# Sums of A quadrants in the output rounds of a fused cross-attention: from GpSimd to VectorE, in the order that the score rounds have

## The reference

```
a = layer_norm(ctx, gamma, beta)
Q, K, V = x @ Wq.T, a @ Wk.T, a @ Wv.T          # split into heads
attn = softmax(mask(Q K^T / sqrt(64)))
out = x + tanh(gate) * ((attn V) @ Wo.T)
```

## Time and profile before

| | |
|---|---|
| median of three executions | 1596.22 us |
| profiled execution, its own time | 1599.35 us |
| its span, first to last instruction | 1597.5 us |
| mean granted TensorE clock | 0.989 |
| TensorE matmuls busy | 1545.4 us (97%) |
| VectorE busy | 1147.4 us (72%), 1298 instructions |
| ScalarE busy | 862.4 us (54%) |
| GpSimd busy | 357.1 us (22%), 254 instructions |
| stretch 890 to 1530 us (640 us) | TensorE 637.35, VectorE 473.20, ScalarE 406.19, GpSimd 241.25 us busy |

### The profile page before, as it was taken

The page is one execution under the profiler, slowest core; times in us unless marked ns, Lnnn a source line. Parts: engine busy times, 40 slices in busy tenths (PEclk is TensorE's granted clock), DMA queues, the critical chain, the costliest instruction groups (busy, mean ns, idle before and its releaser), DMA issues.

```text
span 1597.5 us, 20099 instructions
## 1 busy us (share of the span) xinstructions
PE 1545.4 (97%) x7104; PEld 1254.9 (79%) x7104; DVE 1147.4 (72%) x1298; ACT 862.4 (54%) x1832; POOL 357.1 (22%) x254
## 2 busy tenths in 40 slices
PE   6979999999999999999988999999999999999998
PEld 5756778888888888888766888888888888888887
DVE  8644778686868687878677777777777777777763
ACT  3445444443544354445675666666666666666641
POOL 5323100000000000000132444333344333444321
PEclk9989999999999999999998999999999999999999
DMA  5999864444544453545572444443444534445422
GB/s 212 331 385 387 291 211 157 159 158 158 174 155 173 158 181 135 185 144 172 172 227 87 134 152 152 139 136 115 143 142 150 160 113 129 129 145 158 139 71 87
DMA packets 204578, 271.92 MB, mean 170 GB/s; under 512 B 26688, under 2 KB 92352, under 8 KB 204480
## 3 DMA queue, kind: packets, MB, share of 16 engines
q1 hardware_dynamic: 204480, 270.65, 50.9%
HBM read 161.55 MB, written 105.91 MB: 167 GB/s over the span
## 4 chain that ended last, share of the span: by engine, by line
PE 85%; DVE 8%; DMA 3%; ACT 2%; issue 1%; SPq 1%; POOL 0%; DVEq 0%; ACTq 0%
PE banks L987 27%; PE banks L989 26%; PE banks L988 26%; PE banks L1105 3%; DVE a_ring L847 2%; PE banks L1016 2%; DMA m_scratch<-m_stage 2%; DVE c_out L914 2%; DVE parts L854 1%; DMA xq<-x_t 1%; DVE p_parts L932 1%; ACT probs L683 1%; PE banks L1092 0%; SPq L301 0%; ACT a_ring L638 0%
## 5 line engine op out<-in xcount | busy, mean ns | idle before, releaser
L987 PE MATMUL banks<-parts,a_ring 128*128 128x512 f32 x1792 | 712.4, 398 | 2.9 <-issue 1.8
L989 PE MATMUL banks<-parts,a_ring 128*128 128x512 f32 x1792 | 701.0, 391 | 0.0
L988 PE MATMUL banks<-parts,a_ring 128*128 128x512 f32 x1792 | 700.0, 391 | 0.0
L989 PEld LDWEIGHTS banks<-parts,a_ring 128*128 128x128 f32 x1792 | 337.5, 188 | 72.5
L987 PEld LDWEIGHTS banks<-parts,a_ring 128*128 128x128 f32 x1792 | 338.1, 189 | 70.3 <-issue 2.2
L988 PEld LDWEIGHTS banks<-parts,a_ring 128*128 128x128 f32 x1792 | 338.3, 189 | 67.3
L551 POOL TENSOR_TENSOR probs<-probs,row_rec 128x512 f32<-128x512 f32 x128 | 133.6, 1044 | 1084.4 <-DVE row_rec L928 1084.4
L683 ACT ACTIVATE probs<-probs,neg_max 128x64 f32<-128x64 f32 x1024 | 259.3, 342 | 57.7 <-DVE neg_max L919 57.7
L914 DVE TENSOR_TENSOR c_out<-banks,c_out 128x1024 f32<-128x1024 f32 x160 | 195.5, 1222 | 113.7 <-PE banks L989 109.8
L638 ACT CAST a_ring<-a_sum 128x1024 fp32r<-128x1024 f32 x128 | 134.2, 1048 | 223.2 <-PE banks L989 218.6
L847 DVE TENSOR_TENSOR a_ring<-a_sum,a_ring 128x1024 fp32r<-128x1024 f32 x128 | 185.9, 1452 | 87.5 <-ACT a_ring L638 86.5
(11 more groups left out here) (73 smaller groups left out, 1324.0 us busy)
## 6 DMA issues: line engine op xcount, KB each, us to landing
xq<-x_t SPq DMA_DIRECT2D x32, 1024.0 KB, 5.9
s_scratch<-c_out SPq DMA_DIRECT2D x64, 512.0 KB, 3.1
probs<-s_scratch SPq DMA_DIRECT2D x128, 256.0 KB, 3.1
c_out<-x SPq DMA_DIRECT2D x64, 512.0 KB, 4.6
out<-c_out SPq DMA_DIRECT2D x64, 512.0 KB, 3.1
b_raw<-m_scratch SPq DMA_DIRECT2D x29, 1024.0 KB, 6.6
m_scratch<-m_stage SPq DMA_DIRECT2D x16, 1792.0 KB, 13.1
w_raw<-wk_t SPq DMA_DIRECT2D x16, 256.0 KB, 7.2
```

Source lines behind the costliest of these rows:

```text
L987: pe.matmul(to, wl, mh, start=first, stop=False, skip_group_check=joined)
L988: pe.matmul(to, wh, ml, start=False, stop=False, skip_group_check=joined)
L989: return pe.matmul(to, wh, mh, start=False, stop=last, skip_group_check=joined)
```

## The change

The GpSimd copy of `sum_a` and its four calls go away, and VectorE's calls, which stood under `if n < ROUNDS`, hold for every round. P6, P3 and P7 come right behind `split_a_lo` in the steps of P1, P5 and P6. P5 of an output round comes at the very end of the step of P4, behind the units' work and the `split_b_lo` of that step. `add_out` keeps its place ahead of `split_a_lo` in the output rounds.

```diff
-            def sum_a(n, k):
...
-                nc.gpsimd.tensor_tensor(a_sum[:, A_SUM[k]], *sum_operands(n, k)).then_inc(sum_made, 1)
...
-                if k == P5 and n >= ROUNDS:
-                    sum_a(n, P3)
-                if k == P6 and n >= ROUNDS:
-                    sum_a(n, P7)
...
-                if k == P4 and ROUNDS <= n + 1 < 2 * ROUNDS:
-                    sum_a(n + 1, P5)
-                    sum_a(n + 1, P6)
...
                 if s + 1 < STEPS:
                     split_a_lo(s + 1)
-                if n < ROUNDS:
-                    if k == P1:
-                        sum_a(n, P6)
-                    if k == P5:
-                        sum_a(n, P3)
-                    if k == P6:
-                        sum_a(n, P7)
-                    if k == P4 and n + 1 < ROUNDS:
-                        sum_a(n + 1, P5)
-                    if s > 0:
-                        add_out((s - 1) // 7, (s - 1) % 7)
+                if k == P1:
+                    sum_a(n, P6)
+                if k == P5:
+                    sum_a(n, P3)
+                if k == P6:
+                    sum_a(n, P7)
+                if k == P4 and n + 1 < ROUNDS:
+                    sum_a(n + 1, P5)
+                if s > 0 and n < ROUNDS:
+                    add_out((s - 1) // 7, (s - 1) % 7)
...
                 if s >= 14 * (B - 1) + 6:
                     refill(s)
+                if k == P4 and ROUNDS <= n + 1 < 2 * ROUNDS:
+                    sum_a(n + 1, P5)
```

More of the change, by code:

```diff
@@ L553, in _ @@
             for s in range(14 * (B - 1), STEPS):
-                n, k = s // 7, s % 7
-                if k == P5 and n >= ROUNDS:
-                    sum_a(n, P3)
-                if k == P6 and n >= ROUNDS:
-                    sum_a(n, P7)
                 if s == 103:
```

## The result

The changed kernel is slower by 0.3%, a small difference but clear of the noise in both timings. Timed beside the kernel before, its median was 1602.45 us (6 executions, 1598.98 to 1603.97) against 1597.03 us, the ratio 1.0031 with a 95% interval of 1.0018 to 1.0044. A second timing later gave 1601.94 us against 1597.45, ratio 1.0027 [1.0018, 1.0036], that is +4.3 us (2.9 to 5.7). The forecast had been 1602.1 us, +5.9.

The account below looks back on a forecast made before the run. TensorE was taken as nearly full in the steady rounds, waiting only for VectorE's split L932, with VectorE awaited in the hand-over. Terms 4.5 + 1.4 = +5.9 us on the median 1596.22 gave 1602.1 us, range 1598 to 1607.5.

Parts of the forecast that it names:

- Price of a sum: Each sum moved to VectorE adds 1.14 us to a full queue; 64 sums make 73 us of new VectorE time.
- Term 1, P5 and P6: Steady rounds 17 to 30: P5 fits into waiting for TensorE, P6 replaces L847's wait for GpSimd; cost nothing.
- Term 1, P7: Steady rounds, step of P6: split L932 comes 0.20 us later behind `add_out`, paid in full 14 times, 2.80 us.
- Term 1, P3: Steady rounds, step of P5: next `add_out` 0.08 us late in 11 rounds, more in rounds 18, 20, 25; 1.65 us.
- 4.02, with the sum 5.16: Step of P5: microseconds from L847's start until the next VectorE instruction can start, without and with the sum for P3.
- Term 2: Hand-over from score to output rounds, steps 111 to 114: TensorE's restart in step 114 later by 0.8 to 1.4, taken +1.4 us.
- both stops stay, so I leave it: Hand-over: TensorE's two stops remain, about 4.5 and 4.2 us, so the 5.7 us of low clock was left unchanged.
- VectorE busy: VectorE's busy time was to grow by about 73 us, less some 35 of waits gone.
- win back its waits: Rival, hand-over: VectorE's regained waits count, -1.5 us there, L847 of step 112 before 831 us; 1597.5 us, not slower; 15%.
- The waits did not change sides: Rival: the new queue brings L847 or a sum onto a normalisation, up to 0.5 us in 14 rounds; 1609 us; 5%.
- The low clock did not last longer: Rival, hand-over: first stop grows from 3.25 to 4.5 us, longer low clock costs 3 us more; 1605 us; 8%.
- The rule of the skill: Advice to move work off a saturated VectorE, even to GpSimd; its first half would make the sum larger by 73 us.

Follow-up runs that it names:

- P5 ahead of the pair: Changed kernel with the sum for P5 moved from behind the two Wo splits of the step of P4 to ahead of them: 1598.65 us, ratio 1.0009.

## Why the prediction was right

The direction, the place and the mechanism were right. Two terms were too large, and one of them was argued wrongly. That the time was met within half a microsecond (1602.1 against 1602.45) is partly luck: the sum was 5.9 us, of which the traces show 3.6, and the first timing happened to lie above them.

- *Price of a sum, 1.14 us:* right; L822 starts at 946.46, the sum at 947.59 and L907 at 948.73.
- *Term 1, P5 and P6:* nothing, right; no wait of TensorE appears in their steps.
- *Term 1, P7:* right. The split stands 3.41 us behind `add_out` (forecast 3.42, before 3.22), in each of 14 rounds, so 2.8 us. One sum behind the split takes the whole wait away and one more ahead of it lengthens it by all that the split is later (1.26 us).
- *Term 1, P3:* mis-sized, 1.65 us forecast. All stalls together grew by 3.3 us in the first pair of traces, so P3 is left with some 0.5. The step that was off is "4.02, with the sum 5.16", whose starts came from a queue with gaps. In the full queue of the changed kernel the next instruction can start 5.06 us behind L822 (rounds 22 and 25), and in the other rounds `add_out` stands 5.13 behind it (940.19 to 945.32), 0.63 behind the reduction where 0.57 would do; the 0.06 us fit a wait for TensorE, though the profile lists none. Three rounds were to overrun by more than 0.08; one did, the 25th, whose stall is 1.04 us. The late starts of the `add_out` that opens the step of P5, on which the three rested, are not all the kernel's: in the second profile of the kernel before, its idle time in round 18 is 0.33 us and not 0.98. Only round 25 is late again and again, 1.28, 1.59 and 1.44 us in the three profiles of the changed kernel and 1.25 in the second of the one before. There the 0.7 us of idle time ahead of the next `add_out` takes up most of it; with the sum for P3 in that place it is paid. What `add_out` waits for in that round is open; by the code it can be TensorE or the load of x.
- *Term 2:* its steps were right and its end was not. L822 of step 112 starts 4.61 us behind the pair (forecast 4.6), TensorE's restart in that step comes 1.26 us later (1.26), the pair of step 113 takes 2.85 (2.9), and the restart of step 114 comes 1.32 us later (1.4 taken). The step that did not hold is "both stops stay, so I leave it": the stretch from that restart to the one behind ScalarE's copy took 9.7, 8.2 and 9.8 us in the three traces of the changed kernel, 10.55 and 10.1 in the two of the other, with granted clocks of 0.76 to 1.00. The whole hand-over took 39.8 us in the mean (40.27, 38.77, 40.36) against 39.5 (39.77, 39.27), so nearly all of the 1.32 us was given back. Whether the change shortens this stretch or chance did is open; 1.6 us between executions of one kernel is more than the 0.3 in question.
- *The sum:* 5.9 us forecast. The traces give 3.3 for the rest (737.1 less 733.85, of which the stalls are 3.3) and 0.3 for the hand-over, 3.6 us; the medians gave 5.4 (2.9 to 7.0) and 4.3 (2.9 to 5.7). All agree on 3 to 6. The upper end of the range was added up wrong: 1605 and the 3.3 us by which term 1 could be larger make some 1608.4, not 1607.5.
- *VectorE busy:* 73 less 35 was forecast, 32.5 more was measured. The splits of summed operands lost 29.7 us and the two Wo pairs 4.4 (4.58 + 5.07 less 2.36 + 2.85); the splits of quadrants taken as they are lost 1.7 (119.1 to 117.4), and the other 4 to 5 I have not sorted out.
- *The rivals.* VectorE did not win back its waits: L822 of step 112 lies 4.61 us behind the pair and not below 3.2. The kernel with P5 ahead of the pair shows what that would have taken, and that it is 2.3 us. The waits did not change sides, except for 0.5 us in the pair of step 113, which the forecast had. The low clock did not last longer: in the 5.7 us behind the restart of step 112 the mean granted clock was 0.70, 1.00 and 0.60 in the changed kernel and 0.50 and 1.00 in the one before, though the first stop grew to 4.5 us in two of the three traces.
- *The rule of the skill:* by the Trainium skill (Perfetto Trace Analysis, Optimizing Scalar/DVE Operations) it is a saturated VectorE that work is moved away from; read so, its load of 74% was the reason against the move. The runs show that load was not what cost: the same 64 sums on VectorE give 1602.45, 1598.65, 1591.46 or 1590.23 us by their places alone.

What stays open: where the low clock falls in the hand-over, and why `add_out` of the step of P5 is late in round 25.

## What to carry to other kernels

Ask of an instruction that is to change engines what stands behind it in its new queue: in this kernel it cost what it added ahead of the one instruction that the full engine waits for, and nothing behind it or inside a wait that was there anyway, though its engine was 74% busy. The one exception was a sum placed right behind a GpSimd instruction, which stretched it by 0.5 us. Before moving work off GpSimd to end a contention, try to move its start: a GpSimd instruction that began 1.1 to 1.3 us ahead of a VectorE one with two SBUF inputs made that one wait for all of it, and started 2.7 us later it cost nothing (8.6 us of 1597 here; with P5 and P6 moved to VectorE's idle times as well, 10.6).

## What the runs showed of the hardware

- The opening part, the same code in all kernels up to step 111, took from 819.89 to 824.1 us in the profiled executions, 4.2 us of scatter that no change of these kernels made; a place far down the timeline has to be compared from an anchor near it.
- With restarts at the same offsets within 0.04 us, the low clock fell in different places, and the same stretch took 8.2, 9.7 and 9.8 us in three executions of the changed kernel, and 10.1 and 10.55 in two of the kernel before. The execution with 8.2 us had the shorter stops (2.92 and 2.77 us, where the other two had 4.5 and 4.1).
- Of a GpSimd instruction and a VectorE one with two SBUF inputs the second to start was stretched, whichever it was: VectorE's L847 from 1.22 to 2.15 and 2.40 us, GpSimd's sum of step 113 from 2.40 to 3.39.
- GpSimd's sum of 2.40 us beside a VectorE instruction with one input in PSUM (L932) lengthened neither, where beside one with both inputs in SBUF (L847) it added 0.9 to 1.2 us.
